# Stage edges and attention transfers of a three-stage transformer block on one core: transfers by tiles of 128 tokens

## What is computed

```python
xn = _layernorm(x)
return x + attention(xn) + ffn(xn)

# attention: 16 heads of 16, causal linear attention in chunks, and 4 memories
q, k, v = (split(xn @ w.T) for w in (w_q, w_k, w_v))
sq = elu1(q)
a_f, n_f = sq @ fine_memories, sq @ fine_memory_norms          # each memory
out_coarse = (sq @ M) / (sq @ z)                               # their sum
w = softmax(n_f.mean(-1), axis=0)         # needs the mean over a batch's tokens
out_fine = ((a_f / n_f) * w).sum(0)
gprob = sigmoid(relu(coarse_repr @ eg_w1.T + eg_b1) @ eg_w2.T + eg_b2)
memory_output = gprob * out_fine + (1 - gprob) * out_coarse
for each chunk:                            # S: running sum of k (x) v
    out = (mask(q k^T) v + q S) / (mask(q k^T).sum + q z);  S += k^T v
output = (gate * memory_output + (1 - gate) * local_output) @ w_o.T

# ffn: top 2 of 8 experts (F = 176) and a shared expert (FS = 352)
y = sum_e cw[e] * (silu(x @ wg[e].T) * (x @ wu[e].T)) @ wd[e].T + shared(x)
```

## Time and profile before

| what | value |
|---|---|
| median of 3 runs | 674.85 us (672.58 to 675.6) |
| span of the profiled execution, first to last instruction | 683.6 us |
| its time around the span | none is listed |
| busy: PE / DVE / ACT / POOL | 88% / 72% / 50% / 42% |
| stage 1, stage 2, stage 3 | to 221.5, to 384.5, to 683.6 us |
| DMA | 88.60 MB, 130 GB/s in the mean |

### The profile page before, as it was taken

One profiled execution on the slowest core, in us unless ns is written; L12 is line 12 of the kernel. 1 busy time (PEld: TensorE's weight loads), 2 busy tenths in 40 slices (PEclk: granted clock), 3 DMA queues, 4 the chain that ended last, 5 costly groups with the idle time before them and its releaser, 6 DMA issues. The chain is left out here.

```text
span 683.6 us, 23842 instructions
## 1 busy us (share of the span) xinstructions
PE 601.4 (88%) x8665; PEld 500.9 (73%) x8665; DVE 490.6 (72%) x1461; ACT 342.1 (50%) x870; POOL 287.2 (42%) x375
## 2 busy tenths in 40 slices
PE   1999998998995999999999588988989899889995
PEld 0787786887875899999999476766766676667773
DVE  3484565465575677777777566888888888878896
ACT  4538548548544444444444334555555555555542
POOL 2055064074072830000000303567666766666664
PEclk9999999999998899999999756999999999999997
DMA  9025535446156344445554502432443244323120
GB/s 306 34 106 200 198 138 204 164 152 217 74 199 234 113 129 154 152 150 152 156 164 128 156 23 67 131 95 66 144 142 95 66 157 130 95 66 95 34 66 32
DMA packets 62230, 88.60 MB, mean 130 GB/s; under 512 B 8532, under 2 KB 48436, under 8 KB 62132
## 3 DMA queue, kind: packets, MB, share of 16 engines
q1 hardware_dynamic: 52340, 66.61, 29.3%
q0 software_dynamic: 7520, 20.07, 9.3%
q10 hardware_dynamic: 2272, 0.53, 0.4%
HBM read 46.94 MB, written 40.24 MB: 128 GB/s over the span
## 5 line engine op out<-in xcount | busy, mean ns | idle before, releaser
L1703 POOL DMA_INDIRECT yg<-d_grouped_y,from_row x64 | 63.7, 996 | 15.5 <-issue 11.6
L986 ACT ACTIVATE silu<-e_up 128x176 f32<-128x176 f32 x72 | 22.9, 318 | 91.0 <-PE e_up L91 91.0
L89 PE MATMUL e_up<-wb,xb 128*128 x144 | 51.0, 354 | 1.5 <-DVE xb L1009 1.5
L1639 DVE TENSOR_TENSOR probs<-a_ring,causal_s 128x256 f32<-128x256 f32 x128 | 45.2, 414 | 9.3 <-PE a_ring L1400 8.9
L1545 ACT ACTIVATE hid<-a_ring,b 64x128 f32<-64x128 f32 x32 | 11.6, 363 | 79.0 <-PE a_ring L1428 75.8
L1528 ACT ACTIVATE with_mem<-a_ring 128x340 f32<-128x340 f32 x128 | 46.8, 447 | 4.5 <-PE a_ring L1381 4.5
L91 PE MATMUL e_up<-wb,xb 128*128 x144 | 46.9, 326 | 0.0
L90 PE MATMUL e_up<-wb,xb 128*128 x144 | 46.8, 325 | 0.0
L833 POOL TENSOR_TENSOR ticks<-lane 128x1 f32<-128x1 f32 x4 | 2.2, 561 | 97.7 <-DVE slot_i L746 97.7
L1418 PE MATMUL a_ring<-wo,attT 128*128 128x256 f32 x128 | 37.3, 416 | 6.5 <-ACT attT L1537 3.2
L1023 DVE TENSOR_TENSOR h_sb<-e_up,silu 128x128 f32<-128x128 f32 x72 | 21.0, 292 | 29.8 <-ACT silu L986 23.0
(11 more groups left out here) (290 smaller groups left out, 2064.6 us busy)
## 6 DMA issues: line engine op xcount, KB each, us to landing
v<-d_rows SPq DMA_DIRECT2D x77, 128.0 KB, 2.0
d_grouped_y<-y_sb SPq DMA_DIRECT2D x73, 128.0 KB, 1.9
d_v<-v_half SPq DMA_DIRECT2D x8, 544.0 KB
d_q<-halves SPq DMA_DIRECT2D x8, 512.0 KB
d_k<-halves SPq DMA_DIRECT2D x8, 512.0 KB
total<-d_base SPq DMA_DIRECT2D x8, 512.0 KB
out<-total SPq DMA_DIRECT2D x7, 512.0 KB, 3.9
v<-d_v SPq DMA_DIRECT2D x6, 544.0 KB
```

Of the source, the lines that this page charges most:

```text
L89: pe.matmul(out, a[0], b[0], start=start, stop=False)
L1639: dve.tensor_tensor(probs[:, j, :, :], ps[:, 0:4 * CH].rearrange("p (h i) -> p h i", i=CH), causal[:, :].unsqueeze(1).broadcast_to([P, 4, ...
L1703: pool.indirect_dma_start(yg[tile % GATHERS][:, k, :], None, d["grouped_y"], bass.IndirectOffsetOnAxis(ap=c["from"][:, k, tile:tile + 1], ...
```

## The change

Eight edits:

1. The 13 small loads behind the identity go from ACT's list to SP's, between the shared weights and the tokens of batch 1. The shared weights have a semaphore each, and ACT waits for one at a time.
2. Batch 0 is normalized by DVE (8 TENSOR_SCALAR), not by ACT, and DVE's list makes the low part of the first half of xT ahead of the second shared weight's.
3. `table_words` and `token_shifts` come ahead of DVE's last two `sums`; the first two row blocks for stage 2 are fetched (`first_rows`) ahead of the last store of keys, the other two by stage 2.
4. ACT loads the Silu table at the end of stage 1, not at the start of stage 2.
5. SP no longer waits for the stores of `grouped_y` at the end of stage 2; POOL does, ahead of its first gather. DVE makes indices and weights ahead of the last result.
6. The first tile's keys have masks of their own (`mask0`); the rest of the half is masked after the first copies of norms.
7. The first three gathers wait for PE's first scores, keys and values.
8. All of attention's transfers go by tile: at each tile's first state SP loads a tile of the next batch's queries (and, in the first four tiles, two tiles of base), and at its values a tile of values and keys, then stores the output of tile i-2 and loads the base of tile i-4 of the next batch.

Cut to its core (line numbers are of neither file; what is cut away is the renamed semaphores and the old functions' bodies):

```diff
             tokens(0, s_first)
-            sp.dma_start(st_g, ...).then_inc(s_sw, 16)
+            sp.dma_start(st_g, ...).then_inc(s_sw[0], 16)
...
+            for to, source in c["loads"][1:]:
+                sp.dma_start(to, source).then_inc(c["s_load"], 16)
             tokens(1, s_x[1])
...
                         if (s, what) == (1, "k") and b + 1 == B:
                             store_base(b, 0)
+                            first_rows()
                         store_half(b, s, what)
-            for u in range(2):
-                sp.wait_ge(s_sc[u], B // 2 * SCATTERED)
-            sp.wait_ge(s_tailed, 16 * E)
-            sp.wait_ge(s_ready, 1)
-            for j in range(UNROLL):
-                at = sp.value_load(c["start"][0:1, j:j + 1], min_val=0, max_val=E * REGION - P)
-                sp.dma_start(c["xg"][j], d["rows"][bass.ds(at, P), :]).then_inc(c["s_ga"][j], 16)
             store_base(B - 1, 1)
...
+            def first_rows():
+                for u in range(2):
+                    sp.wait_ge(s_sc[u], B // 2 * SCATTERED)
+                sp.wait_ge(s_tailed, 16 * E)
+                sp.wait_ge(s_ready, 1)
+                for j in range(2):
+                    at = sp.value_load(c["start"][0:1, j:j + 1], min_val=0, max_val=E * REGION - P)
+                    sp.dma_start(c["xg"][j], d["rows"][bass.ds(at, P), :]).then_inc(c["s_ga"][j], 16)
...
             act.activation(tick_s, neg[:, 0:1], ACT.Silu)
-            normed(0, 0)
-            act.wait_ge(s_sw, 64)
             shared_high(0)
             shared_high(1)
             xT_high(0, 0)
-            normed(0, 1)
...
             act.activation(c["keep"][:, :], c["gate"][:, :], ACT.Exp, scale=-1.0)
+            act.activation(tick_s, neg[:, 0:1], ACT.Silu)
...
                 norm_stats(0, range(h * TS, (h + 1) * TS), h)
+            for h in range(NS):
+                dve.wait_ge(s_rstd, h + 1)
+                for t in range(h * TS, (h + 1) * TS):
+                    dve.tensor_scalar(xn[0][:, t, :], x_in[0][:, t, :], rstd[:, t:t + 1], shift[:, t:t + 1],
+                                      ALU.mult, ALU.add).then_inc(s_xn, 1)
             shared_low(0)
+            xT_low(0, 0)
             shared_low(1)
-            xT_low(0, 0)
...
                     if b + 1 == B and i == 5:
                         residual(b, 0)
+                        table_words()
+                        token_shifts()
...
-            for q in range(2):
-                sp.wait_ge(s_yst[q], 16 + 8 * SLOTS + (16 if q == 0 else 0))
...
-            act.activation(tick_s[:, :], c["lane"][:, :], ACT.Silu)
...
-            result(SLOTS + 4, 0, SLOTS * 8 + 16)
-
             dve.wait_ge(s_tables, 1)
...
+            result(SLOTS + 4, 0, SLOTS * 8 + 16)
...
-    order = [("mask", 0, 0, r) for r in range(2)] + [("norms", 0, 0, j) for j in range(NB3)]
+    order = [("mask0", 0, 0, r) for r in range(2)] + [("norms", 0, 0, j) for j in range(NB3)]
+    order += [("mask", 0, 0, r) for r in range(2)]
...
             def load_queries(b, t):
+                tok = slice(t * P, (t + 1) * P)
+                sp.dma_start(sq_of[b % 2][:, :, tok], d["q"][b, :, :, tok]).then_inc(s_q[b % 2], 16)
...
+            tiles = [(b, t) for b in range(B) for t in range(NT)]
+            for i, (b, t) in enumerate(tiles):
+                sp.wait_ge(ready["state"], b * STATES + 2 * t + 1)
                 if b + 1 < B:
+                    load_queries(b + 1, t)
+                if i < TS:
+                    load_base(0, 2 * t)
+                    load_base(0, 2 * t + 1)
+                sp.wait_ge(ready["values"], (b * NT + t + 1) * 2)
                 if b + 1 < B:
+                    load_values(b + 1, t)
+                    load_keys(b + 1, t)
+                if i > 1:
+                    store(*tiles[i - 2])
+                if i > 3 and tiles[i - 4][0] + 1 < B:
+                    load_base(tiles[i - 4][0] + 1, tiles[i - 4][1])
...
-                for tile in range(GATHERS):
-                    fetch(tile)
+                for q in range(2):
+                    pool.wait_ge(c["s_yst"][q], 16 + 8 * SLOTS + (16 if q == 0 else 0))
+                pool.wait_ge(ready["scores"], 4)
+                fetch(0)
+                pool.wait_ge(ready["keys"], 1)
+                fetch(1)
+                pool.wait_ge(ready["values"], 2)
+                fetch(2)
```

More of the change, by code:

```diff
@@ L182, in tokens_phase @@
         ps_proj = [ps_g[0], ps_u[0], ps_g[1], ps_u[1]]
-        s_sw, s_swh, s_swl, s_pro = sem("t_sw"), sem("t_swh"), sem("t_swl"), sem("t_pro")
+        s_sw, s_swh, s_swl, s_pro = [sem(f"t_sw{i}") for i in range(4)], sem("t_swh"), sem("t_swl"), sem("t_pro")
         s_wq, s_wqh, s_wql = sem("t_wq"), sem("t_wqh"), sem("t_wql")
@@ L888, in fetch @@
                 sp.dma_start(xg[buf], d["rows"][bass.ds(at, P), :]).then_inc(s_ga[buf], 16)
+            for j in range(2, UNROLL):
+                fetch(slice(j, j + 1), j)
             sp.wait_ge(s_xT, 5)
@@ L1172 @@
 GATHERS = 3
-NO_BANK = ("weights", "qmean", "mexp", "mask", "fine", "rest", "rows", "fold", "state", "coef")
+NO_BANK = ("weights", "qmean", "mexp", "mask0", "mask", "fine", "rest", "rows", "fold", "state", "coef")
 RING = [x for x in ATT_ORDER if x[0] not in NO_BANK]
@@ L1245, in values_there @@
             else:
-                eng.wait_ge(s_v[b % 2], 16 * NS * ((b + 1) // 2))
-        s_bx, s_out = ([sem(f"a_{n}{s}") for s in range(NS)] for n in ("bx", "out"))
+                eng.wait_ge(s_v[b % 2], 16 * NT * ((b + 1) // 2))
+        s_bx, s_out = ([sem(f"a_{n}{t}") for t in range(2)] for n in ("bx", "out"))
         s_yc, s_ysum, s_sum = sem("a_yc"), sem("a_ysum"), sem("a_sum")
@@ L1322, in load_ahead, with load_base @@
-            def load_ahead(b):
-                pieces = [(sq_of[b % 2][:, kc, :], d["q"][b, :, kc, :], s_q[b % 2]) for kc in range(KC)]
-                pieces += [(v_of[:, b % 2, half(s), :, :], d["v"][b, :, half(s), :, :], s_v[b % 2]) for s in range(NS)]
-                for i, (to, source, signal) in enumerate(pieces):
-                    since(sp, ready["local"], (b - 1) * NT + 1 + i)
-                    sp.dma_start(to, source).then_inc(signal, 16)
+            def load_base(b, t):
+                n = b * NT + t
+                if b:
+                    sp.wait_ge(s_out[n % 2], 16 * ((n - NT) // 2 + 1))
+                since(sp, s_bx[n % 2], 16 * (n // 2))
+                sp.dma_start(total[:, t, :], base_src[b, :, t, :]).then_inc(s_bx[n % 2], 16)
@@ L1499, in walk @@
                     t = n
+                    if what == "mask0":
+                        keys_there(act, 0, 0)
+                        act.activation(masked[j][:, :, 0:P], skT[:, :, 0:P], ACT.Copy,
+                                       scale=c["parity"][:, j:j + 1]).then_inc(s_mask0, 1)
+                        continue
                     if what == "mask":
@@ L1581, in walk @@
                     t = n
-                    if what in ("mexp", "coarseT", "keys", "hidden", "outT", "values", "gate", "mask", "rows"):
+                    if what in ("mexp", "mask0", "coarseT", "keys", "hidden", "outT", "values", "gate", "mask", "rows"):
                         continue
@@ L1765, in build @@
         c["s_ga"] = [sem(f"c_ga{i}") for i in range(UNROLL)]
+        c["s_yst"] = [sem(f"c_yst{q}") for q in range(2)]
         c["s_bst"], c["s_hst"] = [sem(f"c_bst{i}") for i in range(NS)], [sem(f"c_hst{i}") for i in range(3)]
```

87 lines of the change are left out of this document (37 added, 50 removed).

## The result

The changed kernel runs in **663.16 us** (median of 4 runs, 660.12 to 664.4) beside 674.2 us of the kernel before (4 runs): ratio 0.9889, 95% interval [0.984, 0.9937]. The two medians alone give 0.9836, just outside that interval; why the ratio lies nearer to 1 the record does not say. So it is 1.1 to 1.6% faster, and 663.0 had been forecast. The span of the profiled execution is 662.6 us (before 683.6). Ratios are from fast runs alone, while a median is that of all runs of its kernel. The forecast's level was right; what follows shows that its terms for the edges and for edit 8 were badly wrong in opposite directions and happened to cancel.

What follows compares the result with a forecast made beforehand. PE was taken to be at its limit nearly everywhere but the two stage edges; -3.3 - 5.0 - 6.4 - 2.0 + 5.1 = -11.6 us, from 674.85 to 663.2, said as 663; range 653 to 672.

Steps and rivals of the forecast that it cites:

- Start: Start of stage 1: PE's second transposes begin at 13.2, not 17.01; -3.3 us, bounds -3.8 and 0.
- the rival on stage 1: The start's 3.3 and half of the first edge's 5.0 are lost in stage 1: 669 us, chance 0.08.
- Edge of stages 1 and 2: Barrier opens at about 217.3, not 221.4 (-4.1), and ACT follows PE sooner (-0.9): -5.0 us, bounds -6.0 and -3.0.
- The first two fetches lie where SP waits: First edge: half of 3.95 us of fetches falls into SP's wait between stores; late scatters cost up to 2 us.
- ACT can follow PE's transposes at once: -0.9: First edge: table load ends before the barrier, saving 0.9 of the 2.6 us between 221.90 and 224.51.
- the table work: First edge: DVE's 2.3 us of table words, moved ahead of the last two sums, hide in 2.31 us of idle time.
- Edge of stages 2 and 3, and the first tile: Barrier opens 1.4 us sooner and DVE's 5.04 us of idle time goes: -6.4 us, bounds -1.4 and -8.
- the trickle: First tile of attention: scores after the first 42 of 64 trickle while base and gathers fill the DMA engines; DVE idles 5.04 us.
- The rival: First tile: scores trickle because PE starves for its own instructions, whatever the data transfers do; 670.2 us, chance 0.2.
- Boundaries: Batch boundaries: PE's norms wait 1.7 us for the last queries, three times; +5.1 us, bounds +1.5 and +9.
- First tiles and beat: Attention: smaller loads shorten the first tiles, -2.0 us (bounds 0, -4); time per tile unchanged, 0 (bounds -4.6, +4.6).
- The slower rival: Attention: each tile's transfers stall PE, 1 us in each of 24 tiles, +24; 687 us, chance 0.07.

Runs made afterwards that it cites:

- e5: The changed kernel again, no further edit, beside the kernel before: 659.46 us, ratio 0.9849.
- e4: The kernel before with edits 1 and 2 alone: 666.72 us, ratio 0.9948.
- e1: The kernel before again, no edit, with a profile of its own: 668.26 us, ratio 0.9987, span 668.7.
- e11: The changed kernel without edit 8 (edits 1 to 7 alone), same kernel as e3 in a later group: 662.84 us, ratio 0.9903.
- e3: The changed kernel without edit 8 (edits 1 to 7 alone): 662.99 us, ratio 0.9918.
- e8: On top of e2, the next batch's values come in two transfers of 544 KB, behind the values of tiles 1 and 5: 653.01 us, ratio 0.9745.
- e2: The changed kernel with the next batch's queries loaded one tile sooner: 652.0 us, ratio 0.9747.
- e6: The kernel before with edit 8 alone, and the next batch's queries one tile sooner than in edit 8: 658.17 us, ratio 0.9825.
- e10: As e8, but the two 544 KB transfers of values go behind the values of tiles 2 and 6: 652.43 us, ratio 0.9726.
- e12: On top of e11, transfers as long, but both pieces of queries go out at the locals of tiles 0 and 1: 659.81 us, ratio 0.9858.
- e9: As e8, but the two 544 KB transfers of values go behind the locals of tiles 2 and 3, as in the kernel before: 653.32 us, ratio 0.9742.
- e7: On top of e2, SP's first two fetches for stage 2 come behind stage 1's last two stores: 653.27 us, ratio 0.975.

## Why the prediction was right, and where it was not

The level came out right, and so did the gain by the medians, -11.0 us against -11.6 forecast. By the ratio it is -7.5 us (-4.2 to -10.8 by the interval) and in e5 -10.1 us (-7.6 to -12.6), so the gain may well have been forecast too large, and that the level fits so well is in part luck. The parts did not come out. In us of a kernel of 669 us (one ratio point of 0.001 is 0.67 us; differences of two ratios are good to some 3 us):

| term | forecast | measured | from |
|---|---|---|---|
| start (edits 1, 2) | -3.3 | -3.5; 3.0 in the trace | e4, e1 |
| edges, masks, gathers (3 to 7) | -11.4 | -3 | e11 less e4 |
| edit 8 as a whole | +3.1 | -3.6 (-1.9 by the first pairing less e3) | e5 less e11 |
| of it boundaries | +5.1 | +6.5 to 7 | e5 less e8 and e2 |
| of it the rest (first tiles, beat) | -2.0 | -11.7; -11.4 | e6; e2 less e3 |

**Start.** Right, mechanism and size. The first four TENSOR_SCALAR took 1.38 us and not 1.2, and the second shift was ready at 10.74 and not 10.53. The rule on a shared port (the Trainium skill, SBUF — State Buffer), by which this term would have been -2.6, does not show at that size: of the 1.2 us POOL's chain lost 0.2, and the 1.38 us are not the port's, since the second four took as long with POOL's chain over. The rule is for a two-port mode, and no run shows which mode these operations ran in. Nothing on the way to the end of stage 1 ate the gain, so the rival on stage 1 fell in that half.

**Edge of stages 1 and 2: forecast -5.0, measured -1.2 to -1.7** (from the end of stage 1 on PE to its first product: 8.37 us in e1, 8.73 in e4, 7.17 in e5, 7.06 in e11). Two steps failed, and the premise of a third was an event of one execution. "The first two fetches lie where SP waits" was wrong: the scatters landed late, so they run from 205.95 to 207.45 and push both last stores out; the bound given for it, up to 2 us, was the case. And "ACT can follow PE's transposes at once: -0.9" gained nothing, since the next thing late was already there. PE loads its own first word of expert numbers into a register between transposes and product (line 945 of the changed kernel, count, duration in ns, start):

```profile
L945 PEldq TENSOR_LOAD <-pack_i x1: 827/827/827, 210.6 to 210.6; - x1
```

and 937 in e1:

```profile
L937 PEldq TENSOR_LOAD <-pack_i x1: 492/492/492, 214.9 to 214.9; - x1
```

From its start to the product it is 1.5 and 1.2 us, and the product waits for it, table load or not. The trace of before held this row, and I looked only at busy engines.

The third is the table work, which was to bring DVE's end 2.2 us forward, under the idle time of 2.31 us. That cover is not in e1, and in the changed kernel the last sums follow the table work at once, at 203.37. Nor was there so much to win: DVE's last additions end 3.47 us behind PE's last product in the first profile, but 0.98 us in e1 and 0.73 in the changed kernel. So moving the table work gave about 0.25 us. What the edge did gain lies behind DVE's end, where SP has two fetches fewer: 4.93 us from there to the first transposes in e1, 3.45 in the changed kernel.

**Edge of stages 2 and 3, and the first tile: forecast -6.4, measured -1.4 and -0.5.** The barrier was right to the digit (2.90 to 1.53 us). The 5.04 us of the trickle were priced as a property of the kernel, but e1 shows the same transfers in flight, the scores in one piece and DVE without that idle time. That one execution was slower also in its stage 1 (PE's last product there ends at 215.42, in e1 at 207.70). Neither the forecast's cause (data transfers) nor edits 6 and 7 can then be credited. The rival had it better: the stall was longer in the profiled execution than in others, and the 8.8 us between span and median, which spoke for it, should have weighed more. What caused the small groups of 1 to 8 scores in that execution stays open.

**Boundaries: +5.1, measured +6.5 to 7.** Right in place (three norms, waits of 2.02, 1.98 and 2.37 us) and right in kind. The wait is 6.4 us in all and not 5.1: the mechanism was right, and the size was off since the last queries' issue to the norms took 2.5 us (443.59 to 446.12) and not 2.2. The fall of the clock behind it, which I kept for the bound, comes on top, and some is taken back elsewhere.

**First tiles and beat: -2.0 and 0, measured -11.7 together.** This is the step that failed most, and to the good. I took the beat with transfers against that without and found 0.16 us, and so had nothing for edit 8 to win. (The bound from it, 24 x 0.2 = 4.6, is a slip: 24 x 0.16 is 3.8, and 24 x 0.2 is 4.8.) The comparison could not show it: the last six tiles, which I took for those without, still had such waits, 8.34 us a tile in e1 against 8.00 in e8. In e1 the tiles from 1 to 30 take 8.57 us in the mean and in e8 7.96, but not evenly: single tiles of 9.7 to 13.3 us stand among many of 7.5 to 8.1. What is lost there is, for the most part, PE's wait for its own next 16 KB of instructions, 18.5 us in e1 and 6.9 in e8, and the clock behind the longest of them. (The first profile, with 10.5 us of such waits, has the same mean of 8.54: there PE waits longer elsewhere, for ACT's `valT` 10.3 us against 7.1, so the waits of one trace do not give the beat by themselves.) Windows of e1 around its longest wait:

```profile
540.00:544.00 4.00, 3.84 (x116) 2.98 (x114) 3.52 (x9) 2.96 (x10) 1.99 (x3) 1.00 0.91 303
544.00:548.00 4.00, 0.90 (x55) 0.68 (x53) 1.50 (x5) 1.41 (x2) 3.54 (x5) 0.86 0.62 213
548.00:552.00 4.00, 3.72 (x23) 3.06 (x23) 2.75 (x9) 1.15 (x3) 0.95 (x1) 0.50 0.25 76
```

I had this mechanism among the rivals, but only for the trickle, and priced it as something that edit 8 would not touch. It is just what edit 8 shortens. The Trainium skill, Runtime: NRT & Kernel Launch, on instruction fetch mechanics, says that an engine's instructions come in blocks of 16 KiB, each while the last is executed, at a cost "mostly hidden". The packets of 16 KB agree; that their cost is hidden does not hold here, with 3.10 to 3.72 us at one boundary in e1, e3, e4 and e11.

The slower rival (0.48 us lost in each tile) went the other way, as its own counter-argument said.

**What is shown and what is argued.** Shown: that transfers by tile, with the queries asked for in time, gain 10 to 12 us and shorten these waits (e6, same order of work on PE; e2 against e3), that one long transfer by itself does not bring the time back (e8 to e10), and that spreading the long ones takes the wait of 3 to 4 us out of the trace (e12), though a gain in time is not clear of noise there. Seen in four traces: that the packet starts late, behind PE's stop. Argued: that it is late because it queues behind the data, and which of the transfers count; no run tried this by itself. Of the remaining 5.9 to 8 us, 1.6 to 2.1 are one wait at the output transposes of the last batch that every trace has, whatever the transfers (in the first profile at 671.57, outside the window). How much of the rest comes from gathers, which no run moved, is open. So is the half clock after the second edge, 20.5 to 30.7 us long in the experiments, which no edit shortened.

## What to carry to other kernels

Before a term is priced on a stall in one profile, take a second profile of the same kernel, or at least ask whether span and median agree: here 5 of 11.6 us rested on an event of one execution, and the cover for another 2.2 did too. Idle time of an engine that no semaphore ended is not nothing; look at the instruction queue's packets and at how many bytes of data stand in front of them, and keep a queue's wait for a landing from bunching the transfers behind it. When transfers are cut to pieces, ask for the last piece one step before the step that waits for all of them.

## What the runs showed of the hardware that I had not expected

- TensorE's own instructions, in packets of 16 KB, can start late when long transfers are bunched on the DMA queues: it stood still for up to 3.72 us in the middle of 64 small matmuls, at the same matmul in four traces (3.39, 3.44, 3.10, 3.72 us in e1, e3, e4, e11), each time with the packet starting 0.7 to 1.4 us behind its stop, and for 0.17 to 0.32 us there in e8, e9 and e12. In the first profile, with base and queries asked for up to 2 us earlier, it was 0.23 us.
- A single transfer of 544 KB cost no measurable time at any of three places (652.4 to 653.3 us against 652.0); where 2 MB were asked for within 7 us, the waits above stood.
- A wait of 2.02 us of TensorE in full flow was followed by 6.8 us at half clock, which with the wait made 3.6 us on two tiles; one of 1.98 us at the next boundary was followed by 3.4 us at half clock.
- A register load took TensorE 0.49 to 0.83 us (e1, changed kernel), and SyncE 0.65 us and 1.3 us to the first transfer by it (e7); at a stage's edge both lie open.
